# The last stage of a four-stage kernel: one tile turned earlier, and one ternary weight made later

## What is computed

```python
def ternary_quant(w):
    scale = jnp.mean(jnp.abs(w)) + EPS
    q = jnp.clip(jnp.round(w / scale), -1.0, 1.0) * scale
    return w + jax.lax.stop_gradient(q - w)
wu = ternary_quant(W_up)
wg = ternary_quant(W_gate)
wd = ternary_quant(W_down)
up = jnp.einsum('bsd,ed->bse', x, wu)
gate = jnp.einsum('bsd,ed->bse', x, wg)
hidden = jax.nn.silu(up) * gate
return jnp.einsum('bse,de->bsd', hidden, wd)
x = x + _L1_ffn_ref(_layernorm(x, axis=-1), L1_ffn_W_up, L1_ffn_W_gate, L1_ffn_W_down)
```

## Time and profile before

| what | us |
|---|---|
| median of 3 runs | 3522.9 |
| lowest and highest run | 3521.65, 3528.39 |
| the profiled execution | 3521.01 |
| its span in the trace | 3519.3 |
| PE busy | 3429.3 (97%) |
| VectorE busy | 1632.3 (46%) |
| ScalarE busy | 863.3 (25%) |
| GpSimd busy | 744.4 (21%) |

### The profile page before, as it was taken

How to read it: one execution, slowest core, us unless ns; L and a number is a source line. 1 busy time by engine, 2 the same in 40 slices (tenths; PEclk the granted TensorE clock), 3 DMA queues, 4 the chain that set the end, 5 groups by cost and what they waited for, 6 DMA issues and landing times.

```text
span 3519.3 us, 43049 instructions
## 1 busy us (share of the span) xinstructions
PE 3429.3 (97%) x16460; PEld 1797.8 (51%) x16461; DVE 1632.3 (46%) x1978; ACT 863.3 (25%) x1256; POOL 744.4 (21%) x709
## 2 busy tenths in 40 slices
PE   7999999999999789999999989999999999999999
PEld 4565565566456333333333346556565565554554
DVE  8764474565466431111111136446255365662651
ACT  2330131032023211111111125335154252220110
POOL 4200500410320012212222220000000002780860
PEclk9999999999999999999999999999999999999999
DMA  7631131132123196899888975436355251430420
GB/s 221 227 100 53 60 90 47 68 101 64 49 68 124 60 377 202 302 379 312 298 299 298 367 255 166 135 129 182 96 164 158 82 162 57 147 139 2 160 90 38
DMA packets 93030, 556.64 MB, mean 158 GB/s; under 512 B 11289, under 2 KB 11425, under 8 KB 74977
## 3 DMA queue, kind: packets, MB, share of 16 engines
q1 hardware_dynamic: 58288, 445.28, 35.2%
q0 software_dynamic: 31392, 93.76, 10.1%
q10 hardware_dynamic: 3216, 15.68, 1.5%
HBM read 517.62 MB, written 40.71 MB: 159 GB/s over the span
## 4 chain that ended last, share of the span: by engine, by line
PE 86%; DMA 5%; DVE 3%; ACT 1%; issue 0%; SPq 0%; POOL 0%; DVEq 0%; ACTq 0%; POOLq 0%
PE PS L966 15%; PE PS L1954 11%; PE PS L2281 10%; PE PS L1113 9%; PE PS L923 8%; PE PS L1978 6%; PE PS L2307 5%; DMA W<-in_W 4%; PE PS L952 4%; PE PS L818 4%; PE PS L835 3%; PE PS L902 2%; PE PS L1049 2%; PE PS L850 2%; PE PS L976 1%; PE PS L1946 1%
## 5 line engine op out<-in xcount | busy, mean ns | idle before, releaser
L966 PE MATMUL PS<-Sb,kvN 121*128 121x400 f32 (+1 forms) x1536 | 536.7, 499 | 0.0
L1954 PE MATMUL PS<-W,hT 128*64 128x512 f32 x2208 | 503.6, 598 | 15.0 <-DMA W<-in_W 14.1
L966 PEld LDWEIGHTS PS<-Sb,kvN 121*128 121x128 f32 (+1 forms) x1536 | 286.7, 190 | 205.9 <-issue 2.4
L2281 PE MATMUL PS<-xh,wq 128*128 128x400 f16 x2048 | 347.1, 333 | 1.8 <-DVE xh L1341 1.8
L2055 DVE TENSOR_TENSOR gu<-PS,bias 128x512 f32<-128x512 f32 x69 | 47.7, 691 | 633.8 <-PE PS L1954 615.6
L923 PE MATMUL PS<-kvT,wkr 128*128 128x363 f32 x1024 | 340.5, 475 | 0.1
L1113 PE MATMUL PS<-wb,ctxl 128*128 128x512 f32 x768 | 331.0, 592 | 0.0
L2237 POOL TENSOR_SCALAR gtq<-stg,thr 128x1024 f16<-128x1024 f32 x96 | 287.3, 3008 | 170.5 <-DMA stg<-in_F 142.9
L1517 POOL TENSOR_TENSOR qrope<-qrope,rt 128x400 f32<-128x400 f32 x156 | 157.5, 1034 | 719.7 <-DVE rt L1379 713.3
L1954 PEld LDWEIGHTS PS<-W,hT 128*64 128x64 f32 x2208 | 154.9, 137 | 302.6 <-issue 293.2
L2281 PEld LDWEIGHTS PS<-xh,wq 128*128 128x128 f16 x2048 | 200.2, 98 | 148.0 <-DVE xh L1341 2.3
(11 more groups left out here) (290 smaller groups left out, 3778.0 us busy)
## 6 DMA issues: line engine op xcount, KB each, us to landing
W<-in_W SPq DMA_DIRECT2D x96, 2048.0 KB, 12.6
stg<-in_F SPq DMA_DIRECT2D x32, 1536.0 KB, 6.4
kvT<-kvT_d SPq DMA_DIRECT2D x64, 726.0 KB, 4.2
kvN<-kvN_d SPq DMA_DIRECT2D x64, 726.0 KB
absin<-in_F POOLq DMA_DIRECT2D x48, 512.0 KB, 3.9
hn<-in_F POOLq DMA_DIRECT2D x48, 512.0 KB, 4.8
wb<-in_WB SPq DMA_DIRECT2D x8, 2560.0 KB, 9.2
wc_h<-in_WC SPq DMA_DIRECT2D x32, 576.0 KB, 6.0
```

Of the source, the lines that this page charges most:

```text
L966: mm = nc.tensor.matmul(PS[:, value_bank(b) + dc, 0:GW], kvN[b % 2][0:k, lc, dc * P:(dc + 1) * P], Sb[b % 2][0:k, lc, :], start=lc == 0, s ...
L1954: mm = nc.tensor.matmul(PS[g * BS:(g + 1) * BS, 2 + u % 2, :], hT2[k][:, c, half * BS:(half + 1) * BS], W2[:, q, o:o + N1], start=c == 0, ...
L2281: mm = nc.tensor.matmul(PS[:, 4 * q + 2 * w + half, 0:HALF], wq[q][:, w, c, :], xh[part][:, c, half * HALF:(half + 1) * HALF], start=c == ...
```

## The change

Two edits in the last stage. The gate weight's 16 early products of chunk 0 are cut in two by a new argument `cs` of `up_gate`: the 8 of the first four slices of the contraction stay behind the turn of tile 5, the 8 of the other four now stand behind the turn of tile 6. And VectorE makes the down weight of chunk 0 behind the low half of tile 6, not ahead of the low half of tile 4. The numbers of instructions stay as they were on each engine.

```diff
--- before.py
+++ after.py
@@ -2168,9 +2168,9 @@
             sp.wait_ge(sem("out"), 16 * MT)
 
         def ffn_vector(dve):
-            quantise_down(dve, 0, 0, 0)
             for m in range(4, MT):
                 low_rows(dve, m)
+            quantise_down(dve, 0, 0, 0)
             quantise_down(dve, 0, 1, 1)
 
             def low(blk, e, q):
@@ -2269,13 +2269,13 @@
                         chunk(blk, 2 * i + q, q)
 
         def ffn_tensor(pe, body=True):
-            def up_gate(blk, e, q, ws=range(2), halves=range(2)):
+            def up_gate(blk, e, q, ws=range(2), halves=range(2), cs=range(KC)):
                 g = blk * EB + e
                 pe.wait_ge(sem("f_q"), 2 * g + 2)
                 if not (isinstance(g, int) and g < 2):
                     pe.wait_ge(sem("f_hid"), g - 1)
                 for w in ws:
-                    for c in range(KC):
+                    for c in cs:
                         for part in range(2):
                             for half in halves:
                                 mm = nc.tensor.matmul(PS[:, 4 * q + 2 * w + half, 0:HALF], wq[q][:, w, c, :],
@@ -2291,7 +2291,9 @@
                     up_gate(0, 0, 0, range(0, 1), range(0, 1))
                 elif m == 5:
                     pe.wait_ge(sem("a_folded"), 4)
-                    up_gate(0, 0, 0, range(1, 2), range(0, 1))
+                    up_gate(0, 0, 0, range(1, 2), range(0, 1), range(0, KC // 2))
+                elif m == MT - 1:
+                    up_gate(0, 0, 0, range(1, 2), range(0, 1), range(KC // 2, KC))
 
             if not body:
                 return between
```

## The result

| | before | after |
|---|---|---|
| median of the runs timed together (20 each) | 3522.78 | 3527.76 |
| lowest to highest | 3517.35 to 3528.39 | 3524.11 to 3530.61 |
| ratio of after to before | | 1.0013, 95% interval 1.0007 to 1.0018 |
| span of the profiled execution | 3519.3 | 3526.6 |

The kernel is slower by 0.13%, some 4.6 us (2.5 to 6.3 by the interval), within the 0.2% that the prediction called the same, and inside its range.

A forecast was written before the change was run, and what follows sets the result against it. PE, busy 97%, was taken as the bound. A 1.05 us gain vanishes in a 3.35 us stall, leaving +2.3; a clock drop adds 1.7, so 3522.9 + 4.0 = 3526.9 us, range 3520.5 to 3532.

The forecast's parts named there:

- The bound and the place of the gain: PE bounds; around the last tile, turning tile 6 mid-products covers a 0.93 us wait, starting the next products 1.05 us earlier.
- The down weight that costs nothing by itself but holds a load: Chunk 0's down weight ends 3.12 us later, delaying chunk 2's load; PE stalls 3.35 us, chunk 2 begins 2.3 later.
- two loads 1.2 us apart: Loads of chunks 2 and 3 issued closer together cost the first nothing; GpSimd still starts 6.65 us after its issue.
- a fast and a slow landing: Bounds on chunk 2's load: landing in 6.1 us takes 0.55 off, landing in 9.9 adds 3.25.
- the landing of 9.9: Rival at chunk 2's load: shared DMA engines delay the first load; stall 6.6 us, up to +7.3, 3530.2; chance 0.05.
- One stall, and behind it PE is the bound again to the end: After chunk 2's stall PE never waits for weights again, and nothing later gives the 2.3 us back.
- 0.7 us of slack at chunk 4: Chunk 4's weights ready at 3036.0, wanted by PE at 3036.7; the slack grows, as GpSimd's 20.5 undercuts PE's 21.67.
- waits at chunks 4 and 6: Sign against the forecast: PE waiting again at these later chunks would prove it wrong.
- The drop of the clock, 1.7: Behind chunk 2's stall PE's clock likely falls to 0.50, costing 1.70 us; stall with drop, +4.0 in all, chance 0.50.
- The case without a drop: Rival at chunk 2: PE stalls but keeps its clock; +2.3 us, 3525.2; chance 0.33.
- The gain that stays: Rival: nothing is late at chunk 2 and the early products' gain remains; -1.05 us, 3521.9; chance 0.08.
- Faster than before: Whole kernel measurably faster, by more than 0.2% or 7.0 us; chance 0.02.

The follow-up runs named there:

- e2: The kernel before with only chunk 0's down weight moved behind the last low half, PE's order as before; ratio to before 1.0019.
- e5: The kernel before, its order on PE kept, with both first down weights made in the stage before; ratio to before 1.0000.
- e4: The changed kernel's order on PE, with both first down weights made in the stage before; ratio to before 0.9997.
- e1: The changed kernel's order on PE only, with VectorE as before, so the down weight stays ahead of the low halves; ratio to before 1.0003.
- e3: The changed kernel with chunk 0's down weight behind tile 4's low half, ahead of those of tiles 5 and 6; ratio to before 1.0006.
- e6: The changed kernel with 9 unused products added on PE ahead of the first block's loop over chunks; ratio to before 1.0017.
- a2: The changed kernel, unaltered, timed and profiled a second time; ratio to before 1.0012.
- e8: The changed kernel with 3 more products on PE, where another run added 9, for 0.5 us of slack at chunk 2; ratio to before 1.0012.
- e7: The changed kernel with VectorE making the previous low half ahead of the present hidden value in the chunk loop; ratio to before 1.0016.

## Why the prediction was right, and where not

**The bound and the place of the gain: right.** PE's first full products moved from 5.85 to 4.93 behind tile 5's turn. The sum had said 1.05, measured are 0.92: the turn of tile 6 starts 2996.91 - 2994.24 = 2.67 behind tile 5's and not 2.57 (2993.2 - 2990.63). In before the turn of tile 6 itself was held a little by tile 4's low half: it starts 3.86 behind tile 5's turn there, and 3.58 in e2 and e5. The prediction took all of the gain for the turn's; 0.29 of it is VectorE's (e4 against e5).

**The down weight that costs nothing by itself but holds a load: right, and it is the cause.** Load 3.23 later against tile 5's turn (forecast 3.12), GpSimd 6.54 behind it (6.65), VectorE 8.52 behind that (8.51), stall 3.17 (3.35), chunk 2 later by 24.49 - 22.11 = 2.38 (2.3; the 22.11 is 3012.74 - 2990.63, worked out for before as in the prediction). e1 has the turn without the late load and loses 0.24 and no more; e2 has the late load without the turn and loses 4.9. That two loads 1.2 us apart don't disturb the first, read from the earlier trace rows, held too (6.3 to landing, 6.5 before). The prices of a fast and a slow landing were a little off, as they set landings against 6.65, which runs to GpSimd's start. And the landing of 9.9 was no evidence for a late first load: it is the second of the pair of the earlier trace rows, whose first landed in 6.5.

**"One stall, and behind it PE is the bound again to the end": wrong.** This is the step that failed. I took 0.7 us of slack at chunk 4 and expected it to grow, because GpSimd's rhythm of before, 20.5 us a pair between its first two starts, is shorter than PE's 21.67. But the 20.5 were no constant of the chain. The next interval in that trace was 3041.66 - 3020.53 = 21.1, which still would have let the slack grow. What took it is a term that the sum put at nothing: the durations of GpSimd's comparisons were carried over from before, where VectorE's low halves fall elsewhere. With PE close behind the weights the second comparison of an even chunk takes 3.65 and not 2.84. So chunk 4's weights, which were to shift by the load's shift alone, are ready (3040.47 - 2994.24) - (3032.90 - 2990.63) = 3.96 later against tile 5's turn and not 3.12 (the load itself came 3.23 later), and the 0.7 in hand is gone at the first pair. From there the weights of even chunks start 21.87 apart, a little more than PE's pair. PE waits 0.19 in each of seven pairs, 1.3 us in all. e3 shows it with a small stall, e6 takes it away with slack. The prediction had named waits at chunks 4 and 6 as a sign that it is wrong, and they are there, though no table of waits shows them.

**The drop of the clock, 1.7: real, but not in this execution.** The profiled run of after kept its clock over a stall of 3.17, as the stretch behind it shows (PEclk is the 1.00 ahead of the last two numbers):

```profile
3019.00:3020.00 1.00, 1.00 (x8) 0.57 (x7) 1.00 (x1) 0.00 (x0) 1.00 (x1) 1.00 0.00 0
```

Its loss of 3.68 is 2.38 + 1.30, where the forecast had 2.3 + 1.7. So in this execution the 4.0 us came near by luck: a loss that the prediction didn't have, 1.3, stood in for one that didn't occur, 1.7. Only e2, a2 and e8 show the loss as it was forecast. The case without a drop was priced at +2.3 and should have been +3.7.

**The rivals.** The gain that stays is out, as is the landing of 9.9. Faster than before was given 2 in 100 and the same 93, and the same it is. In device time the loss of 4.6 us (2.5 to 6.3) holds both the 3.7 and the 4.2 that the two traces of the changed kernel show.

## What to carry to other kernels

When a step is moved because nobody reads its result for long, follow also what its end sets free: here a buffer, and by it a load, a comparison and a weight with under 1 us in hand. A busy bound engine that shows no waits says nothing of how near its suppliers are; work out the slack at the first item behind the change, and ask what the suppliers will meet at their new times. And a supplier's rhythm that was measured with slack must not be taken for its rhythm without, since here GpSimd's comparison took 2.84 or 3.65 us according to what VectorE began beside it.

## What was not expected of the hardware

The granted clock behind a stall of PE of about 3.2 us could fall either way. It stayed at full after 3.17 (after), 3.07 (e6) and 3.43 (e7), and fell to 0.50 after 3.14 (e8), 3.26 (a2) and 3.38 (e2); after and a2 are the same kernel. The Trainium skill (TensorE: Matmul & The Clock Gate, The HAM clock gate) says that the point of the change differs from run to run; after and a2 agree with it. Each fall cost about 1.7 us where it lay wholly in products.

Much shorter stalls did the same. The prediction took the stall of 2.45 that kept the clock in the earlier trace rows for a sign that the border is near. But the same place, untouched by any of the edits, fell in seven of the twelve profiles, after stalls of 2.29 to 2.56, and kept in the other five, after 2.11 to 2.51. One that fell, from e1:

```profile
1580.14 5.35 PE L1954 MATMUL PS<-W,hT 128*64 128x512 f32 x16 [2.41 <-DMA W<-in_W]
```

So over this range the length of the stall alone didn't decide.

A comparison on GpSimd of 128x1024 took 2.84 us alone and also when VectorE began a subtraction of two SBUF tiles 0.8 into it, 3.65 when VectorE began this as it started, and 4.25 when it started in VectorE's down weight with the low half right behind.
